# Axial tables made in the first projection, a shared eighth bank, and loads handed to the stage in front

## What is computed

```python
x = x + attn(layernorm(x))            # causal, 16 heads of 32
x = x + cross(layernorm(x), ctx, pos) # 32 heads of 16, ctx 4 x 512 x 256, no mask
x = x + ffn(layernorm(x))             # its own norms, causal attention with rotary
                                      # tables and biases, then 8 experts, top 2,
                                      # and a shared expert with a gate
```

```python
ang = pos[..., :, None] * freqs        # freqs = 10000 ** (-arange(4) / 4)
out = stack([x1 * cos(ang) - x2 * sin(ang), x1 * sin(ang) + x2 * cos(ang)], -1)
```

## Time and profile before

| what | value |
|---|---|
| three runs | 2473.26, 2477.84, 2487.39 us; median 2477.84 |
| the profiled execution's own time | 2489.01 us |
| its span, first to last instruction | 2487.3 us |
| TensorE, VectorE, ScalarE, GpSimd busy | 88%, 52%, 37%, 17% of the span |
| mean granted TensorE clock | 0.924 of 2.4 GHz |
| read from HBM, written | 181.55 MB, 102.50 MB |

### The profile page before, as it was taken

How to read it: one execution, slowest core, us unless ns; L and a number is a source line. 1 busy time by engine, 2 the same in 40 slices (tenths; PEclk the granted TensorE clock), 3 DMA queues, 4 the chain that set the end, 5 groups by cost and what they waited for, 6 DMA issues and landing times. The chain is left out here.

```text
span 2487.3 us, 32520 instructions
## 1 busy us (share of the span) xinstructions
PE 2184.4 (88%) x11159; PEld 1390.2 (56%) x11159; DVE 1288.3 (52%) x2847; ACT 911.8 (37%) x1696; POOL 417.3 (17%) x320
## 2 busy tenths in 40 slices
PE   7969999777488999998599599996999999899998
PEld 5855665555322333333477356654788877656565
DVE  4316656388577887874697365553432323222221
ACT  3224444344346666665233254343422221011111
POOL 0000000046400101110266000000100000033332
PEclk9987999888879999998799699988999999899999
DMA  5456554245554544432454666425211214333331
GB/s 186 174 182 145 131 125 114 99 147 192 203 116 101 121 108 119 100 89 50 146 197 182 171 146 150 105 68 205 94 47 39 68 43 188 142 62 60 63 62 39
DMA packets 138854, 297.21 MB, mean 119 GB/s; under 512 B 24962, under 2 KB 27140, under 8 KB 137668
## 3 DMA queue, kind: packets, MB, share of 16 engines
q1 hardware_dynamic: 115556, 243.74, 33.3%
q10 hardware_dynamic: 14400, 32.77, 4.6%
q0 software_dynamic: 8736, 18.62, 3.9%
HBM read 181.55 MB, written 102.50 MB: 114 GB/s over the span
## 5 line engine op out<-in xcount | busy, mean ns | idle before, releaser
L1024 ACT ACTIVATE cross_c_prob<-bank 128x512 f32<-128x512 f32 x512 | 277.8, 593 | 167.9 <-PE bank L887 160.3
L1056 DVE TENSOR_REDUCE cross_c_row_max<-bank 128x2 f32<-128x1024 f32 x256 | 301.0, 1211 | 70.5 <-PE bank L860 67.5
L1379 PE MATMUL bank<-moe_hT,moe_w 128*128 128x512 f32 x1056 | 260.0, 404 | 2.2 <-DVE moe_hT L1616 2.2
L1379 PEld LDWEIGHTS bank<-moe_hT,moe_w 128*128 128x128 f32 x1056 | 205.7, 196 | 46.7 <-DVE moe_hT L1616 2.6
L887 PE MATMUL bank<-cross_c_q_stack,cross_c_k_stack 56*128 56x512 f32 x512 | 167.7, 456 | 37.3 <-ACT cross_c_prob L1024 32.0
L1467 PE MATMUL bank<-moe_w_e,moe_hT_e 128*128 x624 | 194.3, 465 | 2.7 <-DMA moe_w_e<-in_experts_packed 2.3
L1052 DVE CUSTOM_DVE_ANT_0 rotary_c_masked<-bank,later 128x128 f32<-128x128 f32 (+3 forms) x256 | 119.7, 487 | 120.9 <-PE bank L860 119.8
L1052 DVE CUSTOM_DVE_ANT_0 first_c_masked<-bank,later 128x128 f32<-128x128 f32 (+3 forms) x256 | 119.4, 487 | 111.6 <-PE bank L860 110.8
L1024 ACT ACTIVATE rotary_c_prob<-bank 128x512 f32<-128x512 f32 (+3 forms) x256 | 109.2, 437 | 160.7 <-PE bank L890 158.4
L860 PE MATMUL bank<-cross_c_k_stack,cross_c_q_stack 48*128 48x512 f32 x512 | 129.6, 498 | 41.6 <-DMA cross_c_k_stack<-qk_parts 30.5
L1024 ACT ACTIVATE first_c_prob<-bank 128x512 f32<-128x512 f32 (+3 forms) x256 | 108.8, 437 | 148.3 <-PE bank L890 146.0
(11 more groups left out here) (323 smaller groups left out, 4099.2 us busy)
## 6 DMA issues: line engine op xcount, KB each, us to landing
moe_w_e<-in_experts_packed SPq DMA_DIRECT2D x8, 2176.0 KB, 8.3
qk_parts<-first_p_parts SPq DMA_DIRECT2D x32, 512.0 KB, 2.6
qk_parts<-cross_p_parts SPq DMA_DIRECT2D x32, 512.0 KB, 2.7
qk_parts<-rotary_p_parts SPq DMA_DIRECT2D x32, 512.0 KB, 2.7
first_c_q_stack<-qk_parts SPq DMA_DIRECT2D x48, 256.0 KB, 4.4
first_c_k_stack<-qk_parts SPq DMA_DIRECT2D x48, 256.0 KB, 7.1
cross_c_q_stack<-qk_parts SPq DMA_DIRECT2D x192, 64.0 KB, 2.3
cross_c_k_stack<-qk_parts SPq DMA_DIRECT2D x192, 64.0 KB, 2.3
```

What stands on the lines that cost most here:

```text
L1024: nc.scalar.activation(prob[:, n % PROB_SLOTS, 0 : S - q0], psum[bank_scoreT[n % N_SCORET]][:, 0 : S - q0], ACT.Exp).then_inc(s.exp_done, 1)
L1056: nc.vector.tensor_reduce(row_max[:, g % 2, m, j - 1 : j + 1], c.banks[:, first : first + WIDE, :], AX_X, ALU.max).then_inc(s.max_done, 1)
L1379: last = nc.tensor.matmul(psum[bank][:], weights(pa, f, k), hT[p % 2][:, pb, k, :], start=m == 0, stop=m == len(steps) - 1)
```

## The change

1. Stacks. `load_stack` becomes a function of the module, and the projection calls it while it is still at work: in `first` and `rotary` for stacks 0 and 1, in `cross` for 0, 1 and 2, at q tiles (2, 1), (2, 3) and (3, 1) as (batch, tile). The stack buffers live through all attention stages, and the semaphores `stack_loaded0` to `3` are not cleared between stages (`CARRIED`), so that the waits count on. The core loads only the stacks that are left, before it goes on as it did.
2. Rows and weights. `xt` slot 0 and `raw` slot 0 also live on. The core of one attention calls `load_next` at group GROUPS - 2: rows of batch 0 and the q weights of the next projection, or in the rotary core the rows x3 for the experts. The next stage waits on `rows_here` and `raw_here`.
3. Axial tables. Positions of all four batches come in one load, and `pos`, `angle`, `angle_steps` and `trig` run in the first projection, in each batch in front of q tile 1 and 2, sine and cosine behind the last v tile. Tables of all four batches are kept in `axial_cos` and `axial_sin` until the rotary stage begins. The cross projection has none of this work, and no waits for it.
4. Banks. `bank_scoreT` and bank 7 become one pool of three banks for scoresT tiles, transposed maxima and output tiles. `share_banks` walks through the order of the work when the kernel is built and writes down for each use its bank and what frees it.

The diff, cut to its core:

```diff
+def load_stack(sp, a, batch, g):
+    t = Attention(a.kind)
+    h0 = (g % t.groups) * HEADS_AT_ONCE * t.dh
+    slot = g % STACK_SLOTS
+    for stack, w, order in ((a.q_stack, 0, (0, 1, 0)), (a.k_stack, 1, (0, 0, 1))):
+        src = a.scratch[bass.ds(batch, 1), w, h0 : h0 + HEADS_AT_ONCE * t.dh]
+        for half in range(t.halves):
+            for i, part in enumerate(order):
+                ...
+                sp.dma_start(stack[slot][r : r + t.dh].bitcast(F32), of_half).then_inc(a.carried.of[f"stack_loaded{slot}"], 16)
+def load_first(sp, a):
+    sp.dma_start(a.xt0[:], a.x[0:S, :].rearrange("(t p) d -> p t d", p=P)).then_inc(a.carried.rows_here, 16)
+    sp.dma_start(*staged_weights(a, 0, a.raw0)).then_inc(a.carried.raw_here, 16)
...
+        self.early_stacks = STACK_SLOTS - 1 if self.cross else 2
...
-            tables = [(freq[:], a.freq), (sign[:], a.sign)]
+        if turning:
+            tables = [(freq[:], a.freq), (sign[:], a.sign), (pos[:], a.pos.rearrange("(b t p) d -> p b t d", p=P, t=TT))]
...
-        ring = [(0, "pos", 0), (0, "angle", 0)] if cross else []
+        POS_AT, ANGLE_AT = 1, 2
+        ring = []
         for bi in range(BODY):
             for m in range(TT):
-                if cross and m == TT - 1 and bi + 1 < BODY:
-                    ring += [(bi + 1, "pos", 0), (bi + 1, "angle", 0)]
+                if turning and m in (POS_AT, ANGLE_AT):
+                    ring.append((bi, "pos" if m == POS_AT else "angle", 0))
...
+        STACK_AT = {at: g for g, at in enumerate(((BODY - 2, 1), (BODY - 2, 3), (BODY - 1, 1))[: t.early_stacks])}
...
-                    load(0)
+                    if not a.after:
+                        load_first(sp, a)
                     load_context(0)
-                    load_weights(0)
-                    for dst, src in tables:
+                    for dst, src in tables if rotary else ():
                         sp.dma_start(dst, src, allow_slow_non_contiguous=True).then_inc(s.table_loaded, 16)
-                    load_weights(1)
-                    load_weights(2)
+                    sp.dma_start(*staged_weights(a, 1, raw[1])).then_inc(s.raw_loaded1, 16)
+                    sp.wait_ge(s.lo_made, 1)
+                    sp.dma_start(*staged_weights(a, 2, raw[0])).then_inc(s.raw_loaded0, 16)
+                    for dst, src in tables if turning else ():
+                        sp.dma_start(dst, src, allow_slow_non_contiguous=True).then_inc(s.table_loaded, 16)
...
+                            if what == "q" and (bi, m) in STACK_AT:
+                                for st in qk_stored:
+                                    sp.wait_ge(st, 16 * (n_qk // 2))
+                                load_stack(sp, a, loop * BODY, STACK_AT[bi, m])
...
-                            if m == TT - 1 and cross and bi + 1 < BODY:
-                                trig(bi + 1)
+                            if m == TT - 1 and turning:
+                                trig(bi)
...
-        bank_score, bank_scoreT = ((0, 1, 2, 3), (4, 5)) if cross else ((0, 1), (2, 3))
+        bank_score, bank_shared = ((0, 1, 2, 3), (4, 5, 7)) if cross else ((0, 1), (2, 3, 7))
...
+            whole(("max", 0), "max_rows", 1)
+            for g in range(GROUPS):
+                for step in range(N16):
+                    n = g * N16 + step
+                    whole(("score", n), "exp_done", n + 1)
+                    if step == MAX_STEP and g + 1 < GROUPS:
+                        whole(("max", g + 1), "max_rows", g + 2)
+                    if projected_at(g, step):
+                        bi, m, third = projected_at(g, step)
+                        if third == 0:
+                            take(("out", bi * TT + m))
+                        if third == THIRDS - 1:
+                            leave(("out", bi * TT + m), "out_made", bi * TT + m + 1)
...
-                    for g in range(3):
-                        load_stack(sp, g)
+                    for g in range(t.early_stacks, 3):
+                        load_stack(sp, a, loop * BODY, g)
...
+                        if g == NEXT_AT:
+                            for st in out_stored:
+                                sp.wait_ge(st, 16 * (TT // 2))
+                            a.load_next(sp)
...
-                        if n >= N_SCORET:
-                            pe.wait_ge(s.exp_done, n - N_SCORET + 1)
+                        free_bank(("score", n))
...
-                sp.dma_start(xt[:], rows(a.x3, 0)).then_inc(s.m_x_loaded, 16)
...
+        first.items["load_next"] = lambda sp: load_first(sp, cross)
+        cross.items["load_next"] = lambda sp: load_first(sp, rotary)
+        rotary.items["load_next"] = lambda sp: sp.dma_start(xt0[:], x3[0:S, :].rearrange("(t p) d -> p t d", p=P)).then_inc(carried.rows_here, 16)
```

227 lines of the change are left out of this document (122 added, 105 removed).

## The result

The changed kernel runs in 2371.80 us (median of 4, 2364.34 to 2372.53) beside 2482.61 for the kernel before (median of 4, 2473.26 to 2494.24) on the same chip: a ratio of 0.9545, 95% interval 0.9496 to 0.9593. The profiled execution took 2364.34 us, its span is 2362.6 and its mean granted clock 0.948; before it was 2487.3 and 0.924. That is more than the medians differ by, 110.8 us: the profiled execution of the changed kernel was the fastest of its four. A second measurement of the same two kernels gave a ratio of 0.9598 (ninth to eleventh experiment), so the gain of a typical execution is some 97 to 111 us.

The account below looks back on a forecast made before the run. TensorE bounds the first projection, a TensorE-VectorE-GpSimd chain the cross projection, loads the core heads. Terms sum to -116.8: profiled 2489.01 to 2372.2 us, median 2477.84 to 2361; range 2328 to 2408.

Parts of the forecast that it names:

- Core heads: Starts of the three cores: early stacks remove waits of 16.3, 15.4 and 16.3 us, -48 (ends -35 and -52).
- rival A: Core heads: the clock stays up and first groups run at 2.4 GHz, 5 us in each core, 2346; chance 0.13.
- Projection and expert heads: Early rows and weights, no table wait: cross projection -12.3, rotary projection -5.5 (ends -3, -6), experts -1.
- Axial tables into the first projection: Transposes and angle matmuls in four batches where TensorE has no slack: +10.6 (ends +8 and +20).
- Axial tables out of the cross projection: Gap before a batch's seventh item shrinks from 12.5 to 4.3 us, three batches: -24.6 (ends -16 and -30).
- The third bank in the cross core: Score tiles no longer wait for exponentials: 1.0 us in each of 31 intervals, -30 (ends 0 and -45).
- rival B: VectorE's row maxima replace the exponentials as TensorE's wait in the cross core; bank term -8 instead of -36, 2389; chance 0.13.
- The bank in the causal cores: First and rotary cores: the same wait for exponentials shrinks, -3 each, -6 (ends 0 and -14).
- Stack loads in the projections: Stack loads moved into the projections' SP queue ahead of stores of parts: charged 0, other end +10.
- Rival C: Moved transfers collide with sends of maxima or stores; four to six waits costing 5.14 us each, 2387; chance 0.08.
- D: Slower than before: output tiles return the shared bank late, stalling scoresT 36 times; 2595, or 2496 if half wait; chance 0.04.
- E: Stacks or rows arrive no earlier because the stage in front still waits for them at its end; 2478; chance 0.02.

Follow-up runs that it names:

- ninth to eleventh experiment: Changed kernel with the cross projection's next batch turned earlier, alone and with four parts slots, and the changed kernel again, same chip: 2371.87, 2357.23, 2375.89 us.
- early turning, four slots: Changed kernel with next-batch tiles turned behind the fifth cross item, not the seventh, and four slots for query/key parts instead of two: 2357.23 us, ratio 0.9526.
- four slots: Changed kernel with four slots instead of two for the two halves of a query or key tile: 2356.58 us, ratio 0.9515.
- second run: Changed kernel with the early stack loads alone undone, so each core loads all its own stacks: 2409.97 us, ratio 0.9743.
- first run: Changed kernel with the shared bank pool alone undone, products for the exponentials rotating through two banks again: 2402.04 us, ratio 0.9711.
- eighth experiment: Kernel before, run again unedited: 2481.39 us; compared there, the changed kernel with four parts slots and row and stack loads moved on SyncE: 2359.96 us.

## Why the prediction was right, and where it was not

The forecast, 2372.2 for the profiled execution and 2361 for the median, stands beside 2364.34 and 2371.80. The terms came to -116.8, the profiles to -124.7. Only a part of that closeness is earned.

**Core heads, -48.** -16.7, -15.6 and -15.6 make 48.0 before rounding. Undoing the part alone costs 48.3 at the heads. No load of a stack ends an idle time any more. The prediction had named the rows of the maxima, behind stack 2 in the queue, as next late, and so they are, by little: TensorE waits for them in the first group of the rotary core for 1.27 us and in that of the first core for 1.82:

```profile
189.23 0.77 PE L945 MATMUL bank<-stack 104*128 104x512 f32 x1 [1.82 <-DMA stack<-first_c_max_rows]
```

It waits there for 0.9 to 1.8 us in all kernels with early stacks, and for under 0.7 in both profiles of the kernel before and with late stacks.

**The clock at the heads (rival A).** It did not come. The earlier trace rows had 20.92 us of idle time in front of the first core's tiles, now it is 4.67, and the granted clock is 0.50 in both heads above, as it was. The low stretch behind the first tile became shorter, 24.8 us where it was 29.0 and, 10.3 us later, another 3.4, but the first core takes 254.8 us either way. The Trainium skill, "TensorE: Matmul & The Clock Gate", section "HAM oscillation — how this bites in real kernels", has the burst of matmuls behind a wait for data start at the low clock, and keeps the array warm by taking such waits away. The trace agrees with the first half: 4.67 us of idle time are left in front of the first core and the clock is low behind them, and the 5.26 us wait for hT_lo is followed by 5.4 us at 0.50. The second half is not tested at the heads, since the idle time there became shorter and did not go. At the cross projection's first product the clock is at 1.00 for 1.3 us (its first matmul takes 0.47 us where the earlier trace rows has 0.80) and then at 0.50 for 3.4.

**Projection and expert heads, -12.3, -5.5 and -1.** -13.8 (0.4 of it in the first core's own tail), -7.1 and -1.4. Undoing the loads alone cost 5.7 in each of the two projections, undoing the tables alone 5.8 in the cross one; some 2 us of that head came back with neither.

**Axial tables into the first projection, +10.6.** +7.3. The step was right, its size 3 us too high. The rows of the two operations in the first projection:

```profile
L397 PE MATMUL bank<-first_p_posT,first_p_freq 2*128 2x512 f32 x8 | 4.5, 640 | 0.0
L392 PE MATMUL bank<-ident,first_p_pos 128*2 128x128 f32 x16 | 2.4, 272 | 0.0
```

6.9 us in four batches. I had taken 2.04 us for one angle product from a row behind a wait of 3.84 us in the cross projection, where the granted clock was 0.50 (574.5 to 576.6 us); here, with the clock at 0.99 over the stretch, it is 1.1.

**Axial tables out of the cross projection, -24.6: the step that failed.** It said that the seventh item would come after 4.3 us, and it comes after 4.4. It said then: "no engine fills the gap". That sentence was a sum of busy time, VectorE's 26 us in a batch of 32. It missed two things. First, the hole had let the store land, VectorE and GpSimd catch up and TensorE fall behind before the edge. Without it the next batch's ScalarE and VectorE tiles, 3.02 and 3.67 us, come later, by the wait for the store or by the one for GpSimd's product, and TensorE, which has made its products by then, idles for 4.6 to 5.5 us (3.1 to 3.7 in the second profile) instead of 1.5 to 2.8 and then runs at the low clock. Second, even with all of that moved away (early turning, four slots) a batch takes about 35 us: VectorE's busy time is not a constant. It waits for GpSimd's products, and where it need not wait, both engines get slower. The measured gain was 9.5 in one profile and 14.1 in the other, and 13 when undone.

**The third bank in the cross core, -30.** -34.0, and +34.8 when undone. A plain group gained 1.43 us (13.31 to 11.88) where I took 1.0 and where three quarters of the period gave 1.47: the doubt about VectorE (rival B) was misplaced, but only just, since VectorE is now busy for 11.46 of 11.88 us. By that row a further bank could bring a plain group 0.4 us at most (an estimate; no such kernel was run).

**The bank in the causal cores, -6.** 0. The first core takes 254.8 us as before, and undoing the bank made neither causal core longer. The 6.9 us of waits in the earlier trace rows that I took a part of are the weight loads'; these run ahead of the matmuls, and presumably a wait of theirs costs nothing while the matmul in front still runs.

**Stack loads in the projections, 0 with +10 as its end.** +3.7 in the rotary projection, gone in the second run and with four slots. I had held that a late evacuation is covered by four banks; the wait in the trace is ScalarE's, 7.7 us for a store, with hT_hi of the next batch behind it in its order.

**What no term had.** The tail of the cross core, -10.5, and the slow groups of the rotary core, -11.3. Of the tail the bank is 2.3 (first run); the other 8 go with the clock: 0.67 before, 1.00 in every other kernel. In the rotary core the two slow groups give back 13.4, and the first group, which now waits for the maxima's rows, takes 3.5 more in this profile (18.8 against 15.3; 15.7 in the second profile of the changed kernel). In the last group no score tiles are left between the products for the exponentials, and in the kernel before the clock fell there. Yet the kernel with two banks, which has the same waits, kept it. No single part brings the low clock back when undone, so which of them keeps it up stays open; no kernel with two parts undone was run.

Set off against each other: 15.1 too much in the cross body, 6 in the causal bank and 3.7 in rotary were lost, 21.8 came from the tail and the rotary core, nearly all of it where the clock stayed up, and 11 in small pieces from terms that were taken low (the bank, the first projection, the other heads). The range and the sign were right for the reasons given; that the middle fits to 11 us (8 for the profiled execution) is in part luck, since the largest error and the largest gain that nobody forecast in part cancel. Rival C (transfers collide) was right in kind and small: the store's wait, the 1.82 us for the maxima's rows. D and E are refuted: undoing the bank made the kernel slower, and the second run shows that the stacks had come earlier.

**The better version.** Four slots with early turning ran in 2357.23 us (2352.30 to 2361.70) beside the changed kernel's 2375.89 (2359.76 to 2377.84) on one chip, ratios to the kernel before 0.9526 and 0.9598. The intervals overlap, so it is likely rather than settled; four slots alone (0.9515, measured apart from these two) do as well. Shown in the profiles is its 3 to 4 us in the rotary projection.

## What to carry to other kernels

When a hole is taken out of a pipeline, list what ran beside it on every engine before its whole length is written down as gain: here about half of it came back, because the hole had let a store land and two engines catch up before the next batch's tiles. A sum of busy times is no floor for a chain of engines, and for VectorE and GpSimd on SBUF tiles it is not even constant. Undo each part alone at the end: that showed in four runs which terms were real, and that a good total hid one that was 15 us off.

## What the runs showed of the hardware

VectorE and GpSimd, both with two SBUF inputs of 128x512, hold each other up: a sum goes from 0.68 to 1.77 us, a product from 1.29 to 1.74. The Trainium skill, "SBUF — State Buffer", section "Who interferes with whom", says that the two engines share one port pair, that it is an exclusive lock, and that a VectorE instruction with two SBUF inputs contends with a GpSimd instruction that reads SBUF. The timeline above agrees: the sum that starts inside the product ends 0.55 us behind it, and the next product, which starts inside the sum, is 0.45 us longer than one alone.

In the middle of dense work the granted clock fell to its lower level for 17 us, 0.3 us behind the end of a wait of 1.43 us, and the group took 22.1 us at 0.66 where it takes 15.1 at 1.00 (rotary core of the kernel before, timeline and stretch):

```profile
1547.40 0.59 PE L887 MATMUL bank<-rotary_c_q_stack,rotary_c_k_stack 104*128 104x512 f32 x1 [1.43 <-DMA rotary_c_q_stack<-rotary_c_max_rows]
```

```profile
1540.40:1562.50 22.10, 20.67 (x120) 11.80 (x116) 10.09 (x38) 7.98 (x20) 1.74 (x2) 0.66 0.60 135
```

A wait of 1.41 us at the same place in another kernel left the clock at 1.00 (eighth experiment), so the length of the wait does not decide it.

Two profiles of the kernel before differ by 8 us in the rotary core, and two of the changed kernel by 5 in the cross projection, with no difference in the code. A difference of that size between two single profiles is not taken as an effect above unless other runs repeat it.
